# Scatters with the first choice's expert in the row: order of GpSimd's list, two steps moved to VectorE, down products moved behind the blocks

## The reference

```python
h = tok(x, W, b)
h = h + attn(layernorm(h), ...)
t = layernorm(h)
scores, inds = top_k(softmax(t @ Wg.T), 2);  scores /= scores.sum(-1)
y = sum_k scores[k] * down[inds[k]](silu(t @ We_gate.T) * (t @ We_up.T))
shared = (silu(t @ Ws_gate.T) * (t @ Ws_up.T)) @ Ws_down.T
out = h + y + sigmoid(t @ Wsg.T) * shared
```

## Time and profile before

| | us |
|---|---|
| median of 3 runs | 412.72 |
| lowest, highest | 412.58, 422.61 |
| profiled execution | 410.96 |
| its span, first to last instruction | 409.2 |
| mean granted TensorE clock (1 is 2.4 GHz) | 0.956 |
| PE busy | 351.0 (86%) |
| DVE busy | 272.2 (67%) |
| POOL busy | 247.1 (60%) |
| ACT busy | 218.5 (53%) |

### The profile page before, as it was taken

The page is one execution under the profiler, slowest core; times in us unless marked ns, Lnnn a source line. Parts: engine busy times, 40 slices in busy tenths (PEclk is TensorE's granted clock), DMA queues, the critical chain, the costliest instruction groups (busy, mean ns, idle before and its releaser), DMA issues.

```text
span 409.2 us, 10815 instructions
## 1 busy us (share of the span) xinstructions
PE 351.0 (86%) x3434; PEld 318.4 (78%) x3435; DVE 272.2 (67%) x677; ACT 218.5 (53%) x556; POOL 247.1 (60%) x425
## 2 busy tenths in 40 slices
PE   3969999899998999999999887898996998899900
PEld 3869998788787888888878776898995887789800
DVE  4588536556666676677779662674995666676366
ACT  4424436577676777777777561642373544455031
POOL 5675855035565456665656888687570566687453
PEclk9989999999999999999999897999997999999975
DMA  7613665554255334555400001069975344541296
GB/s 247 188 57 89 128 134 113 69 76 64 41 61 68 59 37 58 63 62 60 156 2 3 12 21 30 27 208 372 204 276 142 112 145 120 152 121 57 50 239 185
DMA packets 34387, 44.04 MB, mean 108 GB/s; under 512 B 4682, under 2 KB 29070, under 8 KB 33568
## 3 DMA queue, kind: packets, MB, share of 16 engines
q1 hardware_dynamic: 27118, 31.22, 35.6%
q10 hardware_dynamic: 3762, 5.72, 5.1%
q0 software_dynamic: 3456, 6.45, 4.8%
HBM read 23.46 MB, written 12.31 MB: 87 GB/s over the span
## 4 chain that ended last, share of the span: by engine, by line
POOL 32%; PE 26%; issue 24%; DMA 9%; DVE 6%; SPq 1%; ACT 1%; POOLq 0%; DVEq 0%
PE bank L1238 10%; POOL slots_x L621 6%; POOL on L564 4%; PE bank L1478 3%; DMA xr<-xt 3%; PE pair L1332 3%; POOL att L572 3%; DMA slots_x<-hn2x,slot_u 3%; PE bank L1442 2%; DMA yt<-picked 2%; PE bank L1321 2%; POOL ao L595 2%; POOL parts L546 2%; POOL x_l L533 2%; POOL sq L580 2%
## 5 line engine op out<-in xcount | busy, mean ns | idle before, releaser
L1332 PE MATMUL pair<-vx,PT 113*113 113x128 f32 x512 | 69.0, 278 | 2.6 <-issue 1.6
L1332 PEld LDWEIGHTS pair<-vx,PT 113*113 113x113 f32 x512 | 61.2, 179 | 3.8 <-issue 3.1
L1019 DVE TENSOR_REDUCE smax<-bank 128x8 f32<-128x392 f32 x64 | 36.1, 564 | 38.9 <-PE bank L1311 38.1
L564 POOL TENSOR_TENSOR on<-raw,rz 128x256 f32<-128x256 f32 x32 | 19.9, 621 | 66.9 <-DVE rz L1118 66.7
L683 POOL DMA_INDIRECT picked<-by,bid x40 | 39.2, 981 | 23.7 <-DVE by L1214 13.9
L1321 PE MATMUL bank<-cs,Sm 114*113 114x114 f32 x256 | 41.9, 286 | 6.0 <-DVE Sm L1027 5.7
L814 ACT ACTIVATE PT<-bank 113x456 f32<-113x456 f32 x64 | 35.2, 550 | 18.5 <-PE bank L1321 17.0
L621 POOL DMA_INDIRECT slots_x<-hn2x,slot_u x32 | 33.8, 1055 | 8.8 <-issue 8.0
L1321 PEld LDWEIGHTS bank<-cs,Sm 114*113 114x113 f32 x256 | 30.3, 178 | 9.3 <-DVE Sm L1027 7.3
L1027 DVE TENSOR_TENSOR Sm<-bank,smax 128x392 f32<-128x392 f32 x64 | 35.7, 558 | 0.5
L1250 PE MATMUL bank<-wt_h,x_h 128*98 128x256 f32 x96 | 28.6, 298 | 7.7 <-DVE wt_l L936 6.7
(11 more groups left out here) (194 smaller groups left out, 1098.5 us busy)
## 6 DMA issues: line engine op xcount, KB each, us to landing
bx<-slots_x SPq DMA_DIRECT2D x40, 128.5 KB, 2.1
Qs<-parts SPq DMA_DIRECT2D x48, 98.0 KB
Ks<-parts SPq DMA_DIRECT2D x48, 98.0 KB
we_raw<-we SPq DMA_DIRECT2D x4, 1024.0 KB, 10.7
xr<-xt ACTq DMA_DIRECT2D x13, 294.0 KB, 3.1
slots_x<-pad SPq DMA_DIRECT2D x17, 128.5 KB, 5.7
we_d<-we SPq DMA_DIRECT2D x1, 2048.0 KB, 8.7
yt<-picked SPq DMA_DIRECT2D x10, 196.0 KB
```

The source lines that it names most:

```text
L564: G.tensor_tensor(on[:].rearrange("p b m d -> p (b m) d"), raw[b][:].rearrange("p b m n -> p (b m) n")[:, :, 0:16], bc(rz[b][:].rearrange( ...
L1019: V.tensor_reduce(smax[u % 2][:], score_of(u), AX.X, ALU.max).then_inc(maxed, 1)
L1332: last = T.matmul(bank[4 + b][0:JT, m * 2 * VN:(m + 1) * 2 * VN].rearrange("p (j n) -> p j n", j=2), PT[b][:, m, 0:JT], vx[i % NVX][:, :, ...
```

## The change

- A row of slots_x has 258 values: the token's id, 2 x token, and the expert of its first choice. DVE writes the expert in `one_hot`. In a block the id of the row is 2 x token, plus 1 where the row's first-choice expert is not the block's expert. So nothing is overwritten between the two choices' scatters, and picked holds the two choices of a token next to each other.
- All 32 scatters stand in `SCATTER_AT`, tile by tile with both choices: 8 in halves 75 to 82, then `ez` in half 83, 9 in halves 84 to 92, 15 behind the halves. `ed` stands behind the last of them.
- The low parts `wsh_l` move from GpSimd to DVE, at the end of the same halves.
- The id of a block's rows is made by DVE (`block_id`, between `block_h` and `block_keep`), not copied by GpSimd. For this the block table is worked out on 128 partitions instead of one, and the counts product has 128 columns of output partitions instead of 98.
- `DOWN_LAG` 5 to 4, one more down product in half 91, and BESIDE 11 to 8: in v = 8 to 11 the down products 4 to 7 are done, in v = 12 to 15 none, and eight (8 to 15) behind the blocks instead of five.
- picked is loaded with one DMA for each pair of tiles, with rows of 2 KB.

The diff, cut to its core:

```diff
@@ constants
-ROW = D + 1
+ROW = D + 2
-    k, i = np.divmod(np.arange(TOPK * NT), NT)
-    c[:, C_TOK:C_TOK + TOPK * NT] = k * TOK + i * TT + p[:, None]
+    c[:, C_TOK:C_TOK + NT] = TOPK * (np.arange(NT) * TT + p[:, None])
@@ tables
-        DOWN_LAG = 5
+        DOWN_LAG = 4
-        BESIDE = 11
+        BESIDE = 8
-        FIRST_AT = {59: 0, 61: 1, 63: 2, 65: 3, 66: 4, 68: 5, 70: 6, 72: 7, 87: 8, 88: 9, 89: 10, 90: 11, 91: 12, 92: 13}
-        SECOND_AT = {75: 0, 76: 1, 77: 2, 78: 3, 79: 4, 80: 5, 81: 6, 82: 7}
+        SCATTER_AT = {75: 0, 76: 1, 77: 2, 78: 3, 79: 4, 80: 5, 81: 6, 82: 7, 84: 8, 85: 9, 86: 10, 87: 11, 88: 12, 89: 13, 90: 14, 91: 15, 92: 16}
-        DOWN_AT = {88: 0, 89: 1, 90: 2}
+        DOWN_AT = {88: 0, 89: 1, 90: 2, 91: 3}
@@ gpsimd
-            def scatter(k, t):
+            def scatter(n):
+                t, k = divmod(n, TOPK)
                 j = t // RG
-                if t % RG == 0:
+                if t % RG == 0 and k == 0:
                     pool.wait_ge(slot_known, j + 1)
                     pool.wait_ge(hn2_done, RG * (j + 1))
-                    pool.wait_ge(ids_made, 2)
-                if k == 1 and t % RG == 0:
-                    group = slice(RG * j, RG * (j + 1))
-                    pool.wait_ge(scattered[j % 2], 16 * RG * (j // 2 + 1))
-                    G.tensor_copy(hn2x[:].bitcast(U32)[:, group, D], ids[:, 1, group]).then_inc(ids_moved, 1)
-                    pool.wait_ge(ids_moved, j + 1)
+                    pool.wait_ge(ids_made, j + 2)
...
-                if 54 <= u < 54 + 2 * NS and u % 2 == 0:
-                    n = u // 2 - 27
-                    pool.wait_ge(wsh_hi, n + 1)
-                    cols = slice(n * WSTG, (n + 1) * WSTG)
-                    G.tensor_tensor(wsh_l[:, cols], wsh_raw[:, cols], wsh_h[:, cols].bitcast(F32), ALU.subtract).then_inc(wsh_lo, 1)
...
-            for t in range(NT - 2, NT):
-                scatter(0, t)
+            for n in range(17, TOPK * NT):
+                scatter(n)
             pool.wait_ge(gate_diff, 1)
             G.tensor_tensor(ed[:], euler[:], dl[:], ALU.pow).then_inc(e_exp, 1)
-            for t in range(NT - RG, NT):
-                scatter(1, t)
...
@@ vector
+                if 54 <= u < 54 + 2 * NS and u % 2 == 0:
+                    n = u // 2 - 27
+                    dve.wait_ge(wsh_hi, n + 1)
+                    cols = slice(n * WSTG, (n + 1) * WSTG)
+                    V.tensor_tensor(wsh_l[:, cols], wsh_raw[:, cols], wsh_h[:, cols].bitcast(F32), ALU.subtract).then_inc(wsh_lo, 1)
...
+            def block_id(b, q):
+
+                dve.wait_ge(b_hi, b + 1)
+                need(dve, by_out[q], 2 * b - 2 * q)
+                V.scalar_tensor_tensor(bid[q][:], bx[q][:, D + 1:ROW], eid[:, bass.ds(b, 1)], bx[q][:, D:D + 1],
+                                       ALU.not_equal, ALU.add).then_inc(id_kept, 1)
...
-            blocks(dve, [(2, block_lo), (0, block_h), (-2, block_keep)])
+            blocks(dve, [(2, block_lo), (0, block_h), (0, block_id), (-2, block_keep)])
@@ sync, scalar (loads of picked)
-                for k in range(TOPK):
-                    row0 = k * TOK + g * YG * TT
-                    sp.dma_start(yt[g][:, k], picked[row0:row0 + YG * TT, :].rearrange("(t p) d -> p t d", t=YG)).then_inc(y_in[g], 16)
+                sp.dma_start(yt[g][:].rearrange("p t k d -> p t (k d)"), picked_of(g)).then_inc(y_in[g], 16)
@@ vector, tensor (shared turns)
-                shared_down(v - DOWN_LAG)
+                if v - DOWN_LAG < BESIDE:
+                    shared_down(v - DOWN_LAG)
```

More of the change, by code:

```diff
@@ L146, in build @@
         both = keep("both", [TT, RG + 1, E], BF16)
-        ahead = keep("ahead", [TT, RG + 1, E])
+        ahead = keep("ahead", [128, RG + 1, E])
         chosen_at = keep("chosen_at", [TT, TOPK * RG, E])
         slotr = keep("slotr", [TT, TOPK * RG])
-        run = keep("run", [TT, E])
+        run = keep("run", [128, E])
+        eid = keep("eid", [128, NBLK])
         prow = keep("prow", [1, E], I32)
@@ L278, in build @@
         bid = [ba(f"bid{n}", [BLK, 1], U32) for n in range(BX)]
-        yt = [ya(f"yt{n}", [TT, TOPK, YG, D]) for n in range(NT // YG)]
+        yt = [ya(f"yt{n}", [TT, YG, TOPK, D]) for n in range(NT // YG)]
         bank = [ctx.enter_context(nc.psum_tensor(f"bank{n}", [128, 512], F32)) for n in range(4)]
@@ L325, in build @@
         prow_known, rows_known, e_exp = sem("prow_known"), sem("rows_known"), sem("e_exp")
-        scattered, ids_moved = [sem(f"scattered{n}") for n in range(3)], sem("ids_moved")
+        scattered = sem("scattered")
         wsh_in, we_in, wd_in = sem("wsh_in"), [sem(f"we_in{n}") for n in range(EGU // (2 * STG))], sem("wd_in")
@@ L494, in _ @@
             sp.wait_ge(padded, 16 * (E + 1))
-            for n in range(3):
-                sp.wait_ge(scattered[n], 16 * NT if n == 2 else 16 * NT // 2)
+            sp.wait_ge(scattered, 16 * TOPK * NT)
             for b in range(NBLK):
@@ L904, in _ @@
             for g in FIN_POOL:
-                for k in range(TOPK):
-                    row0 = k * TOK + g * YG * TT
-                    act.dma_start(yt[g][:, k], picked[row0:row0 + YG * TT, :].rearrange("(t p) d -> p t d", t=YG)).then_inc(y_in[g], 16)
+                act.dma_start(yt[g][:].rearrange("p t k d -> p t (k d)"), picked_of(g)).then_inc(y_in[g], 16)
             act.wait_ge(weights_known, 2)
             for g in FIN_POOL:
-                act.wait_ge(y_in[g], 32)
+                act.wait_ge(y_in[g], 16)
                 for q in range(YG):
@@ L1370, in slot @@
                         pe.wait_ge(logit_done, NT)
-                    counts = bank[7][0:TT, E + 1:E + 1 + (RG + 1) * E].rearrange("p (i e) -> p i e", e=E)
-                    T.matmul(counts, up_bf[0:TT, 0:TT], both[:], start=True, stop=True)
+                    counts = bank[7][:, E + 1:E + 1 + (RG + 1) * E].rearrange("p (i e) -> p i e", e=E)
+                    T.matmul(counts, up_bf[0:TT, :], both[:], start=True, stop=True)
                     for i in range(RG):
-                        end = T.matmul(counts[:, i + 1:RG + 1], one_bf[0:TT, 0:TT], bc(both[:, i:i + 1], [TT, RG - i, E]),
+                        end = T.matmul(counts[:, i + 1:RG + 1], one_bf[0:TT, :], bc(both[:, i:i + 1], [TT, RG - i, E]),
                                        start=False, stop=True, skip_group_check=True)
```

100 lines of the change are left out of this document (45 added, 55 removed).

## The result

The changed kernel took 422.24 us (median of 4 runs, 419.71 to 432.06) beside 412.65 of the kernel before in the same job: ratio 1.0255, 95% interval 1.0181 to 1.0328. Run again beside the experiments it took 422.97 (419.08 to 429.41) against 414.73, ratio 1.0158, 1.0097 to 1.0219. So it is slower, by 1 to 3%; whether by more than 2% these runs do not decide. 418 was forecast: the direction was right, the size a little small.

A forecast was written before the change was run, and what follows sets the result against it. No single engine bound it; two chains did, scatters to rows (308.5) and VectorE to weights (311.5). +13.6 - 8.4 + 0 + 0 = +5.2 us on 410.96 gave 416.2, with 1.76 for the median 418 us, range 413.5 to 422.

The forecast's parts named there:

- 1, scatters and ed: Scatters to last low part: VectorE waits for ed behind the scatters; weights ready at 325.1 against 311.50, +13.6 us.
- 2, the earlier part: Before half 75: images give 4.0 us, halves 66 to 75 4.0, id copy 0.35; -8.4, bounds -2.9 and -12.4.
- 3, blocks: The 40 blocks: VectorE's added id instruction hides in 0.47 us of room each; 0, bounds -0.5 and +8.
- 4, tail: Kernel's end: final sums start 2.6 us later but run 2.6 shorter; 0, bounds -3 and +2.6.
- A: Not slower: the part ahead of half 75 gives back all, first scatter before 253; 411 or 409 us; chance 0.13.
- B: Attention gives nothing: moved subtraction lengthens VectorE's chain, half clock returns; +9.6 to +10.7 us, 423; chance 0.12.
- C: VectorE bounds the 40 blocks: 4 to 8 us on top, 424 us; chance 0.11.
- D: VectorE's wait for ed is not long, as scatters issue faster without tile work between; no chance of its own.
- ed near 303: Sign on GpSimd in the trace after: ed stands behind 24 scatters, near 303.
- wait near 14: Sign on VectorE: it waits some 14 us for ed in v = 10, with TensorE idle beside it.
- first scatter near 256: Sign on GpSimd: its run of scatters from half 75 starts near 256, bounds 252 to 261.
- weights the last releaser: Sign at the first block: its turn comes right behind the last low part of expert weights, not behind a load.

The follow-up runs named there:

- before_ed_last: The kernel before with ed alone moved behind its last scatter; 430.74 us, ratio 1.038.
- after_down11: The changed kernel with eleven down products beside the low parts, five last, and DOWN_LAG 5 again; 433.08 us, ratio 1.0405.
- spread_wshpool: The changed kernel with ed ahead in half 88, eight scatters among the last images, shared weights' low parts on GpSimd again; 412.2 us, ratio 0.9975.

## Why the prediction was right in direction and small in size

Measured between the marks that the sum used, in the execution of 419.08 us, the change is +7.5 us (251.6 for 244.1); the sum said +5.2.

- **1, scatters and ed: +13.6 said, +15.1 measured.** From the first of the closely spaced scatters to the last low part: 62.5 us (154.2 - 91.7) for 47.4. The list behind ed was exact, 14.0, and its reason nearly: hs waits for the silu, so the sums that left the turns bought nothing; but ScalarE does not set the turn alone, it waits 0.63 us for VectorE in each. What was short is the train: first scatter to ed's end 48.5 and not 47.0, since not all scatters take 0.96 us; single ones took 1.29 to 1.43, in the other profiles up to 2.55. In the changed kernel's first profile ed ended 49.7 behind the first scatter. The first block follows the last low part by 0.8 us instead of 1.0.
- **2, the earlier part: -8.4 said, -7.3 measured.** The sum was near, its two halves were not, one too small and the other too large: that is luck. The images gave 5.9 (34.9 to 29.0), not 4.0; of that the low parts are 3.5 to 3.8 and the scatters 1.4; 1.0 is a stretch of half clock in the execution of the kernel before that before_ed_last, with the same lists, did not have. Halves 66 to 75 gave 1.4 (15.1 to 13.6), not 4.0. The step that failed is the 2.9 us that I took as lost at half clock: before_ed_last did these halves at full clock, with the same wait of 2.06 us, in 14.4, so the half clock had cost some 0.7 here and was no property of the kernel. And in the changed kernel TensorE waits 2.5 us (1.38 and 1.14), the second time for the silu that I had named as the limit. Against before_ed_last the whole term is -5.6 (first scatter 91.7 for 97.3), not -7.3, and the loss by the change so much larger.
- **3, blocks: 0 said.** From bxT_h to the last copy of a block's result 69.2 us, for 69.4: -0.2. Right.
- **4, tail: 0 said, +0.1 measured.** The final sums start later by 2.6 (401.01 - 389.64 for 390.63 - 381.88, counted from the last copy) and then run 13.4 us for 14.9, and from the last sum to the span's end it is 2.7 for 3.6. Right in both signs. The five together, -7.3, +15.1, -0.2 (the first block's closer start), -0.2 and +0.1, are the 7.5.

**The rivals.** A fell: the first scatter came at 256.8 on the old clock (91.7 behind image 16), not ahead of 253. B fell: the images gave more than I took. The contention that the Trainium skill states (GPSIMD Engine Reference, section 1, Specifications) is there, 0.86 us for 0.46, but on an instruction of GpSimd that had just waited 2.35 us. C fell: the blocks are as long as before. D, given no chance, had none: VectorE waited 13.53 us. Most of what I listed to be seen was seen (ed near 303: 302.76; wait near 14: 13.53; first scatter near 256: 257.17 here; weights the last releaser), but the last low part came 8 us later than 311.5 (319.71) and not 5.

**What the prediction lacked.** It said that "the rows are no longer last" and left them at that. It had taken the rows at their landing, 308.5, and the weights at 311.50, and read two chains 3 us apart. But a block needs its rows loaded, and in the kernel before that load, not the weights, released TensorE, 0.3 us behind the last low part:

```profile
311.77 1.10 PE L1442 MATMUL bank<-cs,bx 128*128 128x128 f32 x4 [2.64 <-DMA bx<-slots_x]
```

So the two chains met, and the rows were a second bound close behind: with ed repaired, bxT_h came 6.3 us earlier where the last low part came 13.2 earlier, and the kernel was no faster than before. And it missed that down products last protect the turns behind a long wait; by the list of after_down11 (16.2 us for 14.0) the change would have cost some 2 us more without them.

So the parts, each by its own run, from one profile a kernel: low parts on VectorE, -3.5 to -3.8 us; ed behind all scatters, +6.3 to +6.4 (bxT_h 155.0 for 148.7 in one train, 147.2 for 140.8 spread); all scatters in one train, +7.8 to +7.9 (bxT_h 155.0 for 147.2 with ed behind, 148.7 for 140.8 with ed ahead); down products last, about 0, or -2 beside the long wait. The copy of the expert's number was not tried alone; what is left over for it between spread_wshpool and the kernel before is 2.5 us of gain (241.6 for 244.1; the ratio, 0.9901 to 1.005, shows none), in which the half clock of that one execution (1.7 us), the end of the wait for landed rows and the down products lie together.

## What to carry to other kernels

An instruction of three microseconds that nobody was waiting for can cost its whole distance in the queue: before moving work past it, ask which list on another engine waits at its semaphore and how long that list is. When a bound is found, measure the one that stands behind it before repairing the first; here each repair alone reached only the time of before, and both together 1% less. Work that leaves a slow stage pays if its new engine was not the one that is full there, even when both engines' instructions get longer beside each other.

## What was not expected of the hardware

- A normalised row of 98x256 on VectorE took 1.95 us beside GpSimd's 128x512 subtraction and 0.76 without it; the other way round, GpSimd's 128x128 difference went from 0.46 to 0.86 beside VectorE's subtraction. With its neighbour's loss, the subtraction cost 1.28 + 1.19 us on GpSimd, where the two met (three times of six), and 0.68 + 0.40 on VectorE.
- TensorE idle for 12 to 13 us resumed at a granted clock of 0.50 and stayed there for 3.7 and 5.2 us (the two profiles of the changed kernel) and 5.6 (after_down11). What that cost depended on how much it had to do in these turns: nothing without the twelve more passes a turn, though full at first (4.98 of 5.00), some 2 us with them.
- The same list of work, with the same wait of 2.06 us on TensorE, ran at half clock in one execution (0.51 in 251 to 257 of the kernel before) and at full clock in another (1.00 in 257 to 263 of before_ed_last). The half clock in one profile is not yet a cost of the kernel.
- The same indirect write of 98 rows took 0.96 us most times and 1.3 to 2.55 now and then, with weight loads under way (2.55 at 300.48 in the first profile of the changed kernel) and without (1.43 at 257.17). With the scatters that were a little longer, the 32 took 32.7 to 35.5 us in the kernels with the new rows, where 32 of 0.96 are 30.7.
